# A graph-attention stage: the source one-hots are cast on GpSimd, and the mask tile gets a third buffer

## The reference

```python
h = x @ Wn.T + bn
e = edge_attr @ We.T + be
a = leaky_relu(sum((h[src] + e) * attn))          # one logit for each edge
m = segment_max(a, dst)
a = exp(a - m[dst])
a = a / (segment_sum(a, dst) + 1e-16)
out = relu(segment_sum(h[src] * a, dst))
```

## Time and profile before

| what | value |
|---|---|
| median of three runs | 4340.02 us |
| the profiled execution's own time | 4305.89 us |
| its span | 4304.1 us |
| attention stage, first mask to last copy out of PSUM | 2644.06 to 3287.2 us |
| granted clock of PE, whole span | 0.915 |

### The profile page before, as it was taken

The page is one execution under the profiler, slowest core; times in us unless marked ns, Lnnn a source line. Parts: engine busy times, 40 slices in busy tenths (PEclk is TensorE's granted clock), DMA queues, the critical chain, the costliest instruction groups (busy, mean ns, idle before and its releaser), DMA issues. The chain is left out here.

```text
span 4304.1 us, 87013 instructions
## 1 busy us (share of the span) xinstructions
PE 3335.9 (78%) x18482; PEld 2452.3 (57%) x18483; DVE 2751.1 (64%) x9374; ACT 1717.5 (40%) x5555; POOL 1143.8 (27%) x908
## 2 busy tenths in 40 slices
PE   5555556888888885999943335899998699998988
PEld 4333335777777774676732224777887344544455
DVE  7999999999898884325478886777665300000453
ACT  1555552234344552102178875777774100000111
POOL 1788888888888000101000000000000000000002
PEclk9999999999999997999955557999999899999998
DMA  2444442556677774666666553433331253543046
GB/s 101 116 109 114 111 111 71 141 166 210 197 214 237 275 282 158 182 198 186 196 189 189 181 166 114 152 122 121 106 108 40 93 194 119 182 154 84 3 173 252
DMA packets 437987, 658.37 MB, mean 153 GB/s; under 512 B 98732, under 2 KB 294167, under 8 KB 437762
## 3 DMA queue, kind: packets, MB, share of 16 engines
q1 hardware_dynamic: 354306, 526.63, 38.9%
q10 hardware_dynamic: 53040, 121.95, 7.8%
q0 software_dynamic: 30544, 8.56, 2.8%
HBM read 440.04 MB, written 216.02 MB: 152 GB/s over the span
## 5 line engine op out<-in xcount | busy, mean ns | idle before, releaser
L1007 POOL DMA_INDIRECT slots<-all_B,put_index x800 | 1051.6, 1315 | 342.9 <-issue 237.8
L1889 POOL MEMSET c_T<- 128x28 f32 x1 | 0.1, 148 | 1983.3 <-POOLq L138 1983.3
L770 DVE TENSOR_SCALAR put_hot<-all_iota_bf,put_words_in 128x125 bf16<-128x125 bf16 x2400 | 443.7, 318 | 3.3 <-DMA put_words_in<-slots 3.3
L2437 DVE TENSOR_TENSOR upd_pre<-upd_po,upd_bias 125x512 f32<-125x512 f32 x25 | 17.3, 692 | 621.5 <-PE upd_po L2368 621.5
L1253 ACT ACTIVATE lm_raised<-lm_hot,srt_words 128x125 f32<-128x125 bf16 x1200 | 356.3, 385 | 83.4 <-DVE lm_top L1168 67.8
L981 PE MATMUL put_ps<-put_right_in,put_left_in 128*128 128x125 f32 x2380 | 340.3, 293 | 51.1 <-ACT put_left_in L840 49.1
L1288 PE MATMUL lm_ps<-lm_v,lm_node 125*128 x1220 | 170.2, 184 | 267.2 <-DVEq L1155 95.4
L2012 PE MATMUL att_ps<-att_right,att_left 128*125 128x125 f32 x2380 | 319.5, 286 | 67.2 <-ACT att_right L2033 63.9
L981 PEld LDWEIGHTS put_ps<-put_right_in,put_left_in 128*128 128x128 f32 x2380 | 300.2, 201 | 76.2 <-ACT put_left_in L840 57.9
L2012 PEld LDWEIGHTS att_ps<-att_right,att_left 128*125 128x125 f32 x2380 | 287.0, 190 | 95.7 <-issue 82.2
L840 ACT CAST put_left_in<-put_hot 128x640 f32 (+1 forms) x238 | 173.8, 730 | 415.0 <-DVE put_hot L770 398.3
(11 more groups left out here) (393 smaller groups left out, 5797.6 us busy)
## 6 DMA issues: line engine op xcount, KB each, us to landing
c_T<-counts SPq DMA_DIRECT2D x255, 312.5 KB, 3.3
pair<-put_T ACTq DMA_DIRECT2D x125, 625.0 KB
hot<-put_hot SPq DMA_DIRECT2D x480, 160.0 KB
att_ring<-hot SPq DMA_DIRECT2D x240, 320.0 KB
gio_T<-pair SPq DMA_DIRECT2D x60, 1250.0 KB, 5.9
all_A<-in_edge_attr_dram SPq DMA_DIRECT2D x100, 448.0 KB
lm_planes<-src_rows SPq DMA_DIRECT2D x123, 320.0 KB, 3.7
counts<-put_T ACTq DMA_DIRECT2D x125, 312.5 KB
```

The source lines that it names most:

```text
L770: ins = v.tensor_scalar(hot[:, h, t, c * S:c * S + P], k["iota_bf"][:, :], words_in[:, j, c, t:t + 1], None, ALU.is_equal)
L1007: nc.gpsimd.indirect_dma_start(slots, bass.IndirectOffsetOnAxis(index[:, C * g + j:C * g + j + 1], 0), stage[:, C * g + j, :], None).then_ ...
```

## The change

ACT's loop keeps only the exponential; it waits for `used` and `powered` in front of each. The casts of the source one-hots go to POOL, in a loop over all 119 groups of the stage that knows no blocks: it waits for the ring slot, then for each part until PE has used the left part of the group before. `far` gets three buffers, and `attend` waits for the powers of group g - 2 instead of g - 1. The `powered` semaphores start at 3 instead of 1, so that the count for g - 2 stays positive.

```diff
+FARS = 3
...
-            far, power = s.sb("far", [L, 2, G * S], bf16), s.sb("power", [L, PARTS, W, P])
-            measured, powered = s.sem("measured"), s.steps("powered", PARTS, PARTS, head=1)
+            far, power = s.sb("far", [L, FARS, G * S], bf16), s.sb("power", [L, PARTS, W, P])
+            measured, powered = s.sem("measured"), s.steps("powered", PARTS, PARTS, head=FARS)
...
                 def widen(g):
-                    r = act.snap(g % RING, min_val=0, max_val=RING - 1)
-                    act.wait_ge(ring.arrived, g + 1)
                     for f in range(PARTS):
                         used.freed(act, g, f)
-                        nc.scalar.copy(left[:, f, :, :], ring.slot(r, lf, W * f, W * f + W)).then_inc(left_ready.sem(f), 1)
-                        if attention:
-                            powered.after(act, g, f)
-                            nc.scalar.activation(right[:, f, :, :], power[:, f, :, :], ACT.Exp).then_inc(right_ready.sem(f), 1)
+                        powered.after(act, g, f)
+                        nc.scalar.activation(right[:, f, :, :], power[:, f, :, :], ACT.Exp).then_inc(right_ready.sem(f), 1)
...
                 def attend(d, g):
-                    powered.freed(dve, g, PARTS - 1)
+                    powered.after(dve, g - 2, PARTS - 1)
                     measure(g + 1)
...
             def _(pool):
-                hooks["pool"](pool)
+                left_ready.begin(pool)
+                last = pool.value_load(k["group_start"][0:1, NB:NB + 1], min_val=1, max_val=NG)
+                with pool.Fori(0, last) as g:
+                    r = pool.snap(g % RING, min_val=0, max_val=RING - 1)
+                    pool.wait_ge(ring.arrived, g + 1)
+                    for f in range(PARTS):
+                        used.freed(pool, g, f)
+                        nc.gpsimd.tensor_copy(left[:, f, :, :], ring.slot(r, lf, W * f, W * f + W)).then_inc(left_ready.sem(f), 1)
+                pool.drain().then_inc(left_ready.sem(PARTS - 1), RING)
```

More of the change, by code:

```diff
@@ L2050, in step @@
                         hooks["act"](act, d - 2)
-                left_ready.begin(act)
-                if attention:
-                    right_ready.begin(act)
+                right_ready.begin(act)
                 blocks(act, step)
-                act.drain().then_inc(left_ready.sem(PARTS - 1), RING)
                 if by_dst:
@@ L2074, in measure @@
                     dve.wait_ge(ring.arrived, g + 1)
-                    v.tensor_scalar(far[:, ds(g % 2, 1), :].rearrange("p a n -> p (a n)"), ring.part(g, rf), -1.0, BIG,
+                    v.tensor_scalar(far[:, ds(g % FARS, 1), :].rearrange("p a n -> p (a n)"), ring.part(g, rf), -1.0, BIG,
                                     ALU.add, ALU.mult).then_inc(measured, 1)
                 def attend(d, g):
-                    powered.freed(dve, g, PARTS - 1)
+                    powered.after(dve, g - 2, PARTS - 1)
                     measure(g + 1)
@@ L2087, in attend @@
                                                          logit[:, ds(G * g + q, 1)],
-                                                         far[:, ds(g % 2, 1), q * S:q * S + P].rearrange("p a n -> p (a n)"),
+                                                         far[:, ds(g % FARS, 1), q * S:q * S + P].rearrange("p a n -> p (a n)"),
                                                          ALU.add, ALU.min)
```

## The result

The changed kernel takes 4356.78 us (median of six runs, 4349.18 to 4362.11), the kernel before 4340.38 on the same chip: a ratio of 1.0038, 95% interval 1.0027 to 1.005. So it is slower, as forecast, but by 16 us where 84 were forecast, less than half.

What follows compares the result with a forecast made beforehand. DVE's chain was taken to pace the attention groups, ACT close behind. Conflict between POOL's casts and DVE's powers (+97.8), less faster first groups (-13.5), gave 4340 + 84 = 4424 us, range 4278 to 4510.

Steps and rivals of the forecast that it cites:

- The bound: Attention stage: DVE's chain paces each group at 3.70 us, with ACT close behind, and also closes each block.
- Part 1: DVE's wait before the mask goes with three buffers: pace 3.70 to 3.16 us a group, together -55 us.
- Part 2: Casts on POOL take 0.38 us each, 1.9 us per group, hidden under the 3.16 us pace.
- rival (c): POOL itself too slow: five casts take 4.2 us, PE waits for the left parts, +47 us, 4387; chance 0.05.
- Part 3: DVE beside POOL: casts and power instructions exclude each other, lifting the pace to 4.74 us; sum over the stage +84 us.
- 0.315 us for each of 470 casts: DVE's price per cast beside POOL: 0.38 less 0.14 hidden plus 0.075; 1.58 us per group after a block's first.
- The 0.075 for lost overlap: Part of the price per cast: power instructions overlap (345 ns each, spaced 0.27 us) and a blocked one does not.
- Rival (b): DVE and POOL lock each other out wholly, nothing hides: 5.44 us a group, +150 us, 4490; chance 0.15.
- The sum: Attention stage: 94 groups going from 3.70 to 4.74 us, +97.8, and 25 first groups to 3.16, -13.5: +84 us.
- Rival (d): Partial conflict cancels the gain, or DVE's wait returns at the exponentials' hand-over: 4340 within 9 us; chance 0.08.
- Rival (a): No conflict between POOL's casts and DVE's powers: -55 us, 4285; the mask's conflict takes back at most 23; chance 0.30.
- The observables: Signs named beforehand in the attention stage's profile: power means, mask-to-mask times, PE's and DVE's standing, small-block lengths.

Runs made afterwards that it cites:

- e2: The changed kernel with two mask buffers and the old wait, so only the casts moved to POOL: 4355.2 us against 4307.93 before (1.0113).
- e7: The kernel before with three mask buffers, plus spare POOL casts of 250 columns that nobody waits for: 4320.95 us against 4307.93 before (1.0033).
- e5: The kernel before with three mask buffers, plus spare POOL casts of 375 columns that nobody waits for: 4381.96 us, 1.0176 to before.
- e8: The kernel before with three mask buffers, plus one semaphore increment behind each DVE power instruction, ten a group: 1.0226 to before.
- e10: The changed kernel with each POOL cast made as two of 125 columns and DVE copying each group's logit columns to a fixed address: 1.0057 to before.
- e6: The changed kernel with only the first 125 of each POOL cast's 250 columns done, the rest left out: 0.998 to before.
- e3: The changed kernel with each POOL cast replaced by a memset of 250 columns and one more semaphore increment on POOL: 0.9971 to before.
- e1: The kernel before with three mask buffers and the later wait alone, casts still on ACT: 4305.34 us against 4307.93 before (0.9997).
- e9: The kernel before with three mask buffers, plus a DVE copy of each group's ten logit columns to a fixed address: 0.9994 to before.
- e12: The changed kernel with casts in halves, five DVE additions a group, and the logit as a bias in ten ACT exponentials: 0.9997 to before.
- e13: The changed kernel with whole casts, five DVE additions a group, and the logit as a bias in ten ACT exponentials: 0.9965 to before.

## Why the prediction was right or wrong

**The bound.** That DVE's chain paces a group was right: in all six kernels with a longer mask-to-mask time (changed, e2, e7, e5, e8, e10) the stage is longer. That it alone closes the block was not: e6 and e3 are 4 and 6 us shorter than e1 with the same mask-to-mask time, and e9 is 1 us longer with a shorter one. What DVE was said to stand for was wrong.

**Part 1, -55 us, was worth -2.4 (e1).** The step that failed reads the 0.54 us as the wait for the last power and lets it go with the wait. The chain was 3.16 us of datapath and a sequencer that needs 3.5 to 3.7 us for the same group (e8, e9); the standing is what the sequencer lacks. The wait itself held the sequencer for 1.0 us in the whole stage. The last power happened to complete there too, and the profile names an inferred releaser. The check that the prediction left out was to ask what stands between the last power and the mask on DVE's sequencer.

**Part 2.** The cast on POOL was estimated at 0.38 us; it takes 0.448 in the mean and 0.383 at least, some of the difference being POOL's own standing. That it is hidden and PE does not wait for it was right (no standing of PE for POOL, and e7), and rival (c) is excluded.

**Part 3: the conflict was right, its size was more than twice too large.** Cast and power hold each other up, and the earlier trace rows alone would have denied it: powers lose beside POOL's casts (e7) and not beside its memsets (e3). The Trainium skill (SBUF — State Buffer, Who interferes with whom) has this rule, and these runs agree with both halves of it. The mis-sized term is 0.315 us for each of 470 casts, 148 us; measured are 62 us, 0.132 for each of these 470 or 0.104 for each of all 595. The prediction took the cast's whole 0.38 us as the time for which it holds DVE.

Only its columns count: 0.83 ns each, as the earlier trace rows gave for the affine selects, are 0.21 us for 250, and the 0.127 us that a power loses are this less 0.08 of hiding. The rest of a cast, 0.18 us if the shortest casts (0.280 us for 125 columns, 0.383 for 250) are extrapolated to no columns, costs the powers nothing. That POOL holds DVE only while it streams fits these three sizes; no run separates it from a longer hold of which more is hidden. The 0.075 for lost overlap measured nothing: in the changed kernel each power still starts 72 to 91 ns before the one in front of it has ended.

Rival (b), DVE standing for the whole of each cast, falls with it. The Trainium skill (SBUF — State Buffer, SBUF: two separate sides) has the shared pair held for the whole instruction while the other fully blocks; 0.127 us beside casts of 0.448 don't agree with that as a price.

**The sum.** Two errors of opposite sign met. The uncontended pace was put at 3.16 us and is 3.5 to 3.7; the contended at 4.74 and is 3.45 to 4.08. Against e1 the powers gain 62 us and the mask 3; 35 us of it go into standing that the sequencer had left in front of the mask (48.2 to 13.6), 7 into an earlier end of the block (DVE's wait for PE, 48.5 to 41.7), presumably since the last exponential no longer queues behind a cast. That leaves 24, of which the stage shows 18.9; 2.4 of gain from e1 make the 16.5.

Told by parts, with e3 for the change without its conflict: forecast were -55 and +139, measured are -8.2 and +24.7. Each part was forecast six to seven times too large, and their sum five times. That the sign came out right owes something to luck, since it hung on the difference of two terms that were both far off. Rival (d), that the conflict about cancels the gain, came nearest, 16 us where it allowed 9; its other branch, that DVE's wait comes back at the exponentials' hand-over, did not happen. Rival (a) is excluded twice, by the longer powers and by e3, where no conflict of the powers is left and 8 us are gained instead of 55.

**The observables.** Powers above 345 ns beside a cast, 345 elsewhere: right. Mask to mask of 4.3 to 5.1 us, and 3.2 for a block's first group: wrong, it is 3.44 to 4.08 but for one interval, and 3.5 to 3.8 for nearly all first groups (3.77 in the block shown). The 50.9 us gone "in any case": it went, but by the conflict filling it, and not in e1. PE's standing up by 84 us: wrong, 63.9 to 64.6; PE's part grows inside its matmul groups (busy 319.5 to 331.3) instead. Small blocks at 21 us: 20.24.

## What to carry to other kernels

A wait that the profile names in front of an instruction is not proof that removing it helps: where an engine issues many short instructions with computed addresses, first ask whether its sequencer could have issued earlier. The trace tells it where the instruction that takes the wait starts later than the end of what it waits for, and a few added semaphore increments test it in one run. The casts that were moved to GpSimd are paid for by DVE's two-input instructions by the columns that GpSimd reads beyond some 95, so memsets cost these instructions nothing and short casts nearly nothing, and what the cost does to the time depends on whether DVE's datapath or its sequencer paces. And two parts of a change that look additive may not be: here the third buffer is worth 2.4 us alone and 33 us beside the casts, because it lets a delayed datapath catch up: the wait that it moves held DVE for 1.0 us in the one case and for 45 in the other.

## What the runs showed of the hardware

- DVE's scalar_tensor_tensor of 125 columns, with two SBUF inputs, takes 344 ns (median, e1); one that meets a POOL cast of 125, 250 or 375 columns takes 0.025, 0.127 or 0.232 us more (e6, changed, e5). Over all casts that is 0.023, 0.104 and 0.176 us for each. Beside POOL memsets of 250 columns it loses nothing (343 ns in the mean, e3), while the mask, a tensor_scalar on bf16, takes 521 ns instead of 494.
- A semaphore increment costs DVE's sequencer 0.1 us (spacing of the powers 0.26 to 0.353 us, e8). A register operation takes 53 to 136 ns, 93 in the median, two for each power. With the loop's branch and the operations in front of the mask that is enough to leave DVE's datapath idle for 0.54 us between two groups.
- A POOL cast from bf16 to f32 takes 0.383 us at least for 250 columns (mean 0.448 beside DVE), 0.280 at least and 0.34 in the mean for 125, 0.497 at least and 0.56 in the mean for 375.
- Ten exponentials of 125 columns with the logit as a bias take 387 ns each on ACT and come 0.30 us apart (e12, e13).
- The stages ahead of attention differ by 23.5 us between two executions of the same code, more than the whole effect of the change, so only the stage's own length could be compared between profiles.
